# Loading x in a two-layer graph attention kernel: two 1 MB loads per turn from ACT's queue, in place of eight of 256 KB from SP's

## The reference

```
h = relu(layernorm(x))
q, k, v = h @ Wq + bq, h @ Wk + bk, h @ Wv + bv          # 8 heads of 64
x = x + softmax(q k^T / 8 + mask(adj)) v
h = relu(layernorm(x))
q, k, v = h @ Wq1^T, h @ Wk1^T, h @ Wv1^T
rel = adj^T * (q k^T);  rel = rel / norm(rel, axis=2)
x = x + rel v
```

## Time and profile before

| | us |
|---|---|
| median of 3 runs | 2515.74 |
| lowest and highest | 2510.83, 2517.51 |
| the profiled execution | 2514.58 |
| its span, first to last instruction | 2512.8 |
| mean granted clock of TensorE | 0.995 of full |

### The profile page before, as it was taken

The page is one execution under the profiler, slowest core; times in us unless marked ns, Lnnn a source line. Parts: engine busy times, 40 slices in busy tenths (PEclk is TensorE's granted clock), DMA queues, the critical chain, the costliest instruction groups (busy, mean ns, idle before and its releaser), DMA issues.

```text
span 2512.8 us, 53411 instructions
## 1 busy us (share of the span) xinstructions
PE 2426.2 (97%) x19252; PEld 1293.3 (51%) x19252; DVE 1417.6 (56%) x4432; ACT 1691.9 (67%) x4108; POOL 1296.9 (52%) x1159
## 2 busy tenths in 40 slices
PE   5999999999999999999999999999999999999986
PEld 2455455555555555555555555555555555555543
DVE  4455665555655555665555665555665555665543
ACT  4677766767766766766776766776766776766762
POOL 2555555545555555555555555555555555555541
PEclk9999999999999999999999999999999999999998
DMA  6565665665765666665666665667655766665652
GB/s 176 112 129 124 145 135 119 134 141 125 148 132 117 139 133 132 139 133 121 143 127 139 140 136 117 143 127 139 142 134 117 143 126 140 142 129 122 126 106 68
DMA packets 938792, 329.13 MB, mean 131 GB/s; under 512 B 885920, under 2 KB 886176, under 8 KB 938528
## 3 DMA queue, kind: packets, MB, share of 16 engines
q1 hardware_dynamic: 936272, 323.35, 61.9%
q10 hardware_dynamic: 2256, 2.36, 0.4%
HBM read 73.93 MB, written 33.55 MB: 43 GB/s over the span
## 4 chain that ended last, share of the span: by engine, by line
PE 84%; DMA 6%; ACT 4%; DVE 3%; POOL 2%; issue 1%; SPq 0%; ACTq 0%; DVEq 0%; POOLq 0%
PE RB L670 38%; PE PB L670 32%; PE S L736 6%; PE O L670 6%; DMA h1t<-h_halves 4%; POOL h_halves L354 2%; ACT h L407 1%; DMA h0t<-h_halves 1%; ACT h_halves L414 1%; DVE k_st L589 1%; ACT k_st L452 1%; PE RB L690 1%; DMA probs_t<-halves 0%; ACT probs L467 0%; DMA x_in<-in_x_dram 0%
## 5 line engine op out<-in xcount | busy, mean ns | idle before, releaser
L368 POOL TENSOR_TENSOR halves<-probs,halves 128x512 f16<-128x512 f32 x512 | 594.3, 1163 | 610.0 <-ACT halves L475 610.0
L467 ACT ACTIVATE probs<-masked,neg_max 128x256 f32<-128x256 f32 x1024 | 510.6, 500 | 280.5 <-DVE neg_max L604 280.5
L604 DVE CUSTOM_DVE_ANT_0 masked<-S,mask 128x256 f32<-128x256 f32 x1024 | 385.9, 419 | 172.6 <-PE S L736 172.5
L354 POOL TENSOR_TENSOR h_halves<-h,h_halves 128x512 f16<-128x512 f32 x256 | 295.4, 1160 | 196.5 <-ACT h_halves L414 196.5
L670 PE MATMUL PB<-h0t,wq 128*128 128x512 f16 x1536 | 357.2, 383 | 35.8 <-DMA h0t<-h_halves 35.7
L670 PE MATMUL RB<-wvt,h1t 128*128 128x512 f16 x1536 | 353.8, 380 | 25.0 <-DMA h1t<-h_halves 25.0
L670 PE MATMUL PB<-h0t,wk 128*128 128x512 f16 x1536 | 353.0, 379 | 0.0
L670 PE MATMUL PB<-wv,h0t 128*128 128x512 f16 x1536 | 352.2, 379 | 0.0
L670 PE MATMUL RB<-h1t,wm 128*128 128x512 f16 x1536 | 347.2, 379 | 0.0
L475 ACT ACTIVATE halves<-probs 128x512 f16<-128x512 f32 x512 | 323.5, 632 | 16.2
L670 PEld LDWEIGHTS O<-v,probs_t 128*128 128x128 f16 x6144 | 248.4, 98 | 126.1 <-DMA probs_t<-halves 7.2
(11 more groups left out here) (70 smaller groups left out, 2888.8 us busy)
## 6 DMA issues: line engine op xcount, KB each, us to landing
x_in<-in_x_dram SPq DMA_DIRECT2D x128, 256.0 KB, 3.5
x_res<-in_x_dram SPq DMA_DIRECT2D x128, 256.0 KB, 3.8
out_dram<-result SPq DMA_DIRECT2D x128, 256.0 KB, 2.5
probs_t<-halves SPq DMA_TRANSPOSE x512, 2.8
h0t<-h_halves SPq DMA_TRANSPOSE x128, 3.2
h1t<-h_halves SPq DMA_TRANSPOSE x128, 3.3
rv<-in_L_gnn_Wq_dram SPq DMA_DIRECT2D x1, 1024.0 KB, 8.3
rq<-in_L_gnn_Wk_dram ACTq DMA_DIRECT2D x1, 1024.0 KB, 5.3
```

Of the source, the lines that this page charges most:

```text
L354: nc.gpsimd.tensor_tensor(h_halves[:, n, 1, :], h[:, n % 2, :], h_halves[:, n, 0, :], ALU.subtract).then_inc(h_low[layer], 1)
L368: nc.gpsimd.tensor_tensor(halves[:, n % RING, 1, :], probs[:, n % 2, :, :].rearrange("p t n -> p (t n)"), halves[:, n % RING, 0, :], ALU.s ...
L467: ins = nc.scalar.activation(probs[:, n % 2, i, :], masked[:, n % 2, i, :], ACT.Exp, bias=neg_max[:, n % 2, i:i + 1], scale=-1.0, accum_ou ...
L604: ins = nc.vector.tensor_tensor_reduce(out=masked[:, n % 2, i, :], in0=S[n % 2][:, i, :], in1=mask[:, i, :], scale=SCORE, scalar=BIG, op0= ...
```

## The change

`LOADS` keeps one step for `x_in`, in slot 1, and one for `x_res`, in slot 14. The steps are picked up in ACT's program, no longer in SP's, and each moves all four tiles, 1 MB, with one DMA. With one DMA in place of four, the condition under which it may start is the one for all four tiles: ACT's `ln_done` of the whole previous pair for `x_in`, and `r_done` of the whole pair before last for `x_res`. VectorE waits once for `x_in` in place of four times. GpSimd waits for all of `x_res` as before, with the smaller count.

```diff
-    LOADS = {13: [("x_res", 0, 0), ("x_res", 1, 0)], 14: [("x_res", 2, 0), ("x_res", 3, 0)],
-             1: [("x_in", 0, -1), ("x_in", 1, -1)], 2: [("x_in", 2, -1), ("x_in", 3, -1)]}
+    LOADS = {1: [("x_in", 0, -1)], 14: [("x_res", 0, 0)]}
...
 (sync)
-                if kind == "x_in" and p > 0:
-                    sp.wait_ge(ln_done[0], TILES * (p - 1) + n + 1)
-                    sp.dma_start(x_in[:, n, :], xv[p][:, n, :]).then_inc(x_loaded[n], 16)
-                elif kind == "x_res":
-                    if p == 1 and n == 0:
-                        sp.wait_ge(setup_done, NSETUP)
-                    need(sp, r_done, NRC * (p - 2) + RELATE.index(("out", n)) + 1)
-                    sp.dma_start(x_res[:, p % 2, n, :], xv[p][:, n, :]).then_inc(res_loaded[p % 2], 16)
-                elif kind == "split":
+                if kind == "split":
...
 (gpsimd)
-                        pool.wait_ge(res_loaded[p % 2], 16 * TILES * (p // 2 + 1))
+                        pool.wait_ge(res_loaded[p % 2], 16 * (p // 2 + 1))
...
 (scalar)
+                if kind == "x_in" and p > 0:
+                    act.wait_ge(ln_done[0], TILES * p)
+                    act.dma_start(x_in[:, :, :], xv[p]).then_inc(x_loaded[0], 16)
+                elif kind == "x_res":
+                    if p == 1:
+                        act.wait_ge(setup_done, NSETUP)
+                    need(act, r_done, NRC * (p - 1))
+                    act.dma_start(x_res[:, p % 2, :, :], xv[p]).then_inc(res_loaded[p % 2], 16)
...
 (vector)
-                    dve.wait_ge(x_loaded[n], 16 * (p + 1))
+                    if n == 0:
+                        dve.wait_ge(x_loaded[0], 16 * (p + 1))
```

More of the change, by code:

```diff
@@ L444, in _ @@
             for kind, n, p in pairs(PLAN):
-                if kind in ("q", "k"):
+                if kind == "x_in" and p > 0:
[6 more added lines that the diff above has]
+                    act.dma_start(x_res[:, p % 2, :, :], xv[p]).then_inc(res_loaded[p % 2], 16)
+                elif kind in ("q", "k"):
                     c = PROJECT.index((kind, n))
```

## The result

The changed kernel takes 2605.64 us (median of 6 runs, 2603.08 to 2622.16) against 2514.55 us for the kernel before on the same chips (6 runs): it is slower by 91 us; the forecast was 2592 us, 77 us slower. The ratio of the means of the runs is 1.0381, 95% interval 1.0349 to 1.0413.

What follows compares the result with a forecast made beforehand. TensorE, busy 97% of the span, was taken to bound the kernel. Only the `x_res` load's meeting with unit 4's transpose was priced: 31 x 2.5 = 78 us on 2514.6 us gave 2592 us, range 2509 to 2660 us.

Steps and rivals of the forecast that it cites:

- Nothing to win: TensorE, busy 97%: its 25.0 us of waits for `h1t` stay whatever happens to x; gain from `probs_t` waits taken as 0.
- The issues and waits on ACT cost nothing: Two load issues per turn on ACT, hidden by the ACTIVATE ahead, and their waits: zero; uncovered, 2 x 0.4 us per turn.
- Where `x_res` falls: Behind unit 5's first half on ACT, at 1273.79, together with SP's `probs_t` transpose of unit 4 at 1273.76, 31 times.
- The price of the meeting: Unit 4's `probs_t` transpose lands beyond its 5.83 us of room: TensorE stalls 2.5 us per turn, 31 x 2.5 = 78 us.
- The two meetings of the first 30 us: Early load-transpose meetings in the trace, applied to unit 4: 1.6 us late by one, 4.9 us late by the other.
- The estimate by packets: Unit 4's 1024 packets, mixed with the load's, take 5.3 us in place of 1.0: landing after 7.1 us, 1.3 us late.
- (a): Early meeting: load issued at 13.44 lands in 5.3 us; the transpose issued behind it at 15.2 takes 5.6 us.
- `x_in` without cost: Load behind unit 13's first half on ACT: unit 13's `probs_t` transpose takes 5.6 us of its 7.70; cost zero.
- The near miss: Unit 12's transpose packets are through by 1235.9, the `x_in` load's start at about 1236.1: a miss by 0.2 us.
- Sharing without loss: Rival: DMA engines share queues without loss; unit 4 lands within 6.3 us, total 2514 to 2530 us; chance 0.34.
- Faster: Rival: no transpose stands behind a load any more; if all `probs_t` waits go, 2497 us; chance 0.09.
- Both mix: Rival: the `x_in` load also delays unit 13's transpose, 2.2 us late; 31 x 7.1 = 220 us, 2735 us; chance 0.07.

## Why the prediction was right

**Nothing to win (right).** The wait for `h1t` stayed, 25.0 and 24.9 us, though `x_res` lands sooner than before.

**The issues and waits on ACT cost nothing (right, shown).** An issue takes 0.374 us beside a running ACTIVATE, ACT's busy time did not change, and with the load at slot 16 the same issues give a ratio of 0.9998.

**Where `x_res` falls (right, off by 0.14 us).** Forecast 0.03 us after unit 4's transpose, found 0.11 us before it (median; up to 0.81 us in single turns). The sign mattered little: with the load 0.03 us before the transpose, or at the same time, the landing is 0.55 to 0.6 us earlier.

**The price of the meeting (right within 5%, in part by luck).** It was set at a third of the way from 1.3 to 4.9 us, 2.5 us per turn or 78 us. TensorE's wait before unit 4's product, turns 2 to 32, is 2.40 us in the mean (1.35 to 4.38), 74.5 us in all. The landing time, 8.13 us in the median (7.2 to 9.95), is 0.2 us below the 8.3 that the forecast comes to. The two meetings of the first 30 us did bound it. But "a third of the way" between two single events was a choice and no mechanism. The estimate by packets, which has the two transfers pass side by side and the transpose land after 7.1 us, is not what happens: the load's packets pass first, and the transpose lands 0.8 us behind the load. The load itself takes 7.5 us and not the 5.3 of (a), nor the 5.7 that it takes from slot 16; in the turn shown none of its packets passes before 1251.5, behind those that SP had issued earlier, a delay that the forecast has not. Unit 5 made no second stall, with 7.3 us from issue to landing.

**`x_in` without cost (right, shown by moving it alone).** Unit 13's transpose takes 5.3 us, forecast 5.6; the load takes 6.1 us, just above the 5 to 6 forecast. The near miss held in nearly all turns; unit 12's was late to land in a few (7.4 us in one) and nothing waited.

**Missing from the sum: the clock.** The forecast priced a stall at its length. The stalls also brought the granted clock down from 2.4 to 1.2 GHz in 12 of 31 turns, and 31.2 us of longer matmuls came on top. The bound of 4.9 us per turn covered it by its width and not by its reason. By the median of the runs the miss is 14 us; by the profiled execution, which lies 14 us above that median, 27 us: 4 us too much idle time in the forecast (77.5 against 73.2), and the 31.2 us that it lacked. The other runs bear out the clock's part: those of 2619 and 2622 us had a mean granted clock of 0.983 and 0.982, the four of 2603 to 2607 us 0.986 to 0.990.

**The rivals.** *Sharing without loss* put the landing at 6.3 us at the latest; it was 8.13, the load's grew from 5.3 to 7.5 us as well, and in 31 turns of 31 unit 4 came late. The Trainium skill states on the page "DMA: Bandwidth & Descriptors", section "Queues, rings and completion order", that a DMA engine takes turns between its queues, packet by packet. The trace shows no taking of turns for most of the load: 303 of its packets and 4 of SP's queue pass in the 3 us from 1252 to 1255. Whether packets of the transpose stood ready by then no view shows, so this case neither bears out the rule nor refutes it. *Faster* needed the waits for `probs_t` to go. They stayed: without unit 4's they are 15.5 us, in place of 17.8 before. The wait of GpSimd for `x_res` shrank by 68.6 us and gave TensorE nothing. *Both mix* was a matter of place: at slot 1 the load of `x_in` costs nothing, at slot 3, beside unit 14, it costs 1.6%.

None of the versions is faster than the kernel before; the best of them equal it. What stays open is why the transpose's packets do not start before the load's are nearly through, though its issue is over at 1251.72 in the turn shown: they may stand in line or may not be made yet, and no run tells the two apart. Also open is why two stalls of equal length differ in what the clock does behind them.

## What to carry to other kernels

For each DMA whose result TensorE uses soon, take the room from issue to use out of the timeline. Then look for a bulk load in another queue that goes out with it or shortly before it. Here transposes issued from 0.1 us ahead of such a load to 1.9 us behind it landed 0.8 to 1 us behind it, so the load's own landing time is what the room has to hold. Behind the transpose in the same queue, 3.7 us later in the other one, or with one slot more of room, the load cost close to nothing (0 to 0.3%); 1.8 us later it cost 0.9%, since it then met the next transpose, with 7.0 us of room. In this kernel, whose TensorE is 97% busy, the stalls also cost busy time through the clock: 0.43 us for each us of added idle time (31.2 / 73.2), and 0.2 to 0.45 in the experiments with a loss.

## What the hardware did that was not expected

- **A DMA on ACT goes out before the ACTIVATEs ahead of it.** In three kernels the load went out within 0.15 us of unit 4's transpose in the median, though it stood behind zero, one and two more ACTIVATEs; in the turn shown of the third it was 1.0 us ahead of the last one's start. Only a wait that was still open moved it (to 1.83 us behind the transpose).
- **The meeting holds SP too.** The issue of the transpose behind the one that meets the load takes 4.6 us of SP's time in the median (4.49 in the turn shown) in place of 1.23; the longest issue of the 512 in the changed kernel is 5.36 us:

```profile
L300 SPq DMA_TRANSPOSE probs_t<-halves x512: 1231/1234/5362, 46.6 to 2553.4; - x171
```

- **The load passes first:** the transpose issued within 0.1 us of it, before or behind, gets its packets through when the load's are nearly through. So the cost is not in proportion to the bytes: 512 KB beside the transpose add 3.4 us to it, 1 MB 5.3 us, and four of 256 KB 4.0 us to it and 5.0 to the next.
